# Two 64-row matmuls side by side for the row-maximum scores, and an output added in device memory

## The chip, the cores and the metric

The kernel runs on one core of one Trainium2 chip. The metric is device time in microseconds (us) of one execution. Before the change it is 2181.55 us, the median of three runs (2180.68 to 2182.76).

## The reference

32 samples of 128x1024 float32 pass through four blocks, each of the form x = x + block(layernorm(x)). Cut to what matters:

```
R    = (Wq0 c + bq0) (Wk0 c + bk0)        c: the sample's 128x1024 context; q and k have 64 rows
attn = softmax(R, axis=-1)                1024 x 1024 per sample
x    = x + (attn @ (Wv0 ln(x) + bv0))     block 1
x    = x + (ln(x) * in_scale) @ sign(W).T * out_scale + bias      block 2, scales from a router
x    = x + softmax(ln(x) Wq1 (c Wk1)^T / 32) @ c                  block 3
x    = x + 2 * sum_h score_h * (ln(x) A_h^T) B_h^T                block 4, rank 16, 8 heads
```

## The kernel before

**Stages.** A setup part (until some 130 us) builds products of the weights that all samples share. Then a loop works on three samples at once: iteration k *prepares* sample k (projections, transposes, high and low parts of the operands), does the 1024x1024 *attention* of sample k - 1, and the *chain* of blocks 2 to 4 of sample k - 2. Iterations 3 to 31 are one hardware loop; the first three and the last two are written out. The order of each engine's work is written by hand, and engines wait for one another through semaphores.

**High and low parts.** A 32-bit operand of a product is split into a rounded high part and a remainder, and products are summed from three or four matmuls. `q_hl` holds q's high part in rows 0 to 63 and its remainder in rows 64 to 127; `k_hh` holds k's high part in both halves. `q_m` has a copy of q's high part in rows 64 to 127 (a DMA, L670).

**The row-maximum stage** opens the attention. For each of 8 tiles of 128 queries, `query_scores` (L1114, called at L1183) computes 128x1024 scores with two matmuls (L1125), each 128 rows deep and 512 columns wide, which write the two halves of `scores[t % 2]`. VectorE (DVE) takes the maximum of each row (`row_maximum`, L871 to L876). Query tile t waits for the maximum of tile t - 2. The maxima are transposed (L1222) and enter the second computation of the scores (`key_scores`), from which the exponentials are taken. What is not the row maximum does not depend on these first scores.

**What stands between the query tiles** on TensorE (PE): "key product units" (`keys_through_queries`, L1136 to L1139; three matmuls of 512 columns each, 16 units per sample, the last of the three reads a slot of the ring `m_ring` that SyncE fills from device memory), spread by the table `KW_UNITS` (L611); and the beginning of the chain: transposes of the normalized x (L1105), the gate (L1195, eight products whose outputs are 32 rows each, on four column strips of the array), `fold` (L1216), the router's transpose (L1200), the input scale (L1207), two output scales (L1145).

**The end of a sample.** The last matmuls of block 4 (L1328 to L1334) leave two halves in `shared[0]` and `shared[1]`. VectorE multiplies them by `r_inv[2]`, adds `res` (the sum so far), writes `result` (the same memory as `oscale`) and counts `out_ready` (L1089). SyncE stores `result` to the output (L679). The next iteration's transposes (L1105, at t = 1) write the same `shared` banks, and so wait for `out_ready` (L1187). GpSimd (POOL) waits for `out_ready` too, before it refills `res` with `x1 + bias_rows` (L701). ScalarE (ACT) computes the normalized x for the transposes at the start of the chain (L718, called at L740).

```
for h in range(2):
    last = mm(scores[t % 2][:, half(h)], q_hl[:, t * P:(t + 1) * P], k_hh[:, half(h)], start=True, stop=True)
last.then_inc(maxscores_done, 1)
```

Of the kernel before, what the change touches and what calls it, by code (L numbers as in the profile page):

```python
# [24 lines left out]
P = 128  # L25
# [23 lines left out]
def build(nc, x, ctx_, wq0, bq0, wk0, bk0, wv0, bv0, w_ffn, b_ffn, gate, ics, ocs,  # L49
# [13 lines left out]
    with top:  # L63
# [430 lines left out]
        r_bias = sb("r_bias", [P, 1])  # L494
        r_exp = [sb(f"r_exp{i}", [P, E]) for i in range(2)]
# [107 lines left out]
        out_ready = sem("out_ready")  # L603
        dve_prepare = Steps(sem("dve_prepare"), 2)
# [6 lines left out]
        KW_UNITS = (4, 5, 7, 8, 11, 12, 13, 14, 16)  # L611
# [25 lines left out]
        with nc.Block() as block:  # L637
# [3 lines left out]
            def _(sp):  # L641
# [3 lines left out]
                def body(k, prepare, attend, chain):  # L645
# [31 lines left out]
                    if chain:  # L677
                        sp.wait_ge(out_ready, nth(2, c, 2))
                        sp.dma_start(out[c], result[:, :]).then_inc(stored, 16)  # L679
# [6 lines left out]
            def _(pool):  # L686
# [9 lines left out]
                def body(k, prepare, attend, chain):  # L696
                    b, a, c = k, k - 1, k - 2
                    if chain:
                        pool.wait_ge(x1_ready, nth(2, c, 2))
                        pool.wait_ge(out_ready, nth(2, c - 1, 2))  # L700
                        nc.gpsimd.tensor_tensor(res[:, :], x1[:, :], bias_rows[:, :], ALU.add).then_inc(biased, 1)  # L701
                    if chain:
                        norm_scale(2, c)
                    if prepare:
                        norm_scale(0, b)
                    if chain:
                        norm_scale(3, c)
                    if attend:
                        norm_scale(1, a)

# [4 lines left out]
            def _(act):  # L715
# [20 lines left out]
                def body(k, prepare, attend, chain):  # L736
                    b, a, c = k, k - 1, k - 2
                    if chain:
                        act.wait_ge(xnT_done[3], nth(2, c - 1, 2))
                        normalize(1, c, xn_1, x1)  # L740
# [93 lines left out]
                    if chain:  # L834
# [5 lines left out]
                        nc.scalar.activation(lowT_hi[:, :], shared[1][:, 0:P], ACT.Identity).then_inc(lowT_hi_ready, 1)  # L840

# [4 lines left out]
            def _(dve):  # L846
# [24 lines left out]
                def row_maximum(a, t):  # L871

                    dve.wait_ge(maxscores_done, nth(8, a, t + 1))
# [49 lines left out]
                def body(k, prepare, attend, chain):  # L923
# [6 lines left out]
                    if attend:  # L930
                        row_maximum(a, 1)
                        row_maximum(a, 2)
                    if chain:
# [3 lines left out]
                    if attend:  # L937
                        row_maximum(a, 3)
# [145 lines left out]
                    if chain:  # L1084
                        dve.wait_ge(stored, nth(16, c - 1, 16))
                        dve.wait_ge(lora_scale_ready, nth(1, c, 1))
                        for h in range(2):
                            dve.wait_ge(out_done, nth(2, c, h + 1))
                            nc.vector.scalar_tensor_tensor(result[:, half(h)], shared[h][:, :], r_inv[2][:, :], res[:, half(h)],  # L1089
                                                           ALU.mult, ALU.add).then_inc(out_ready, 1)  # L1090
# [6 lines left out]
            def _(pe):  # L1097
# [16 lines left out]
                def query_scores(a, t):  # L1114
# [9 lines left out]
                    for h in range(2):  # L1124
                        last = mm(scores[t % 2][:, half(h)], q_hl[:, t * P:(t + 1) * P], k_hh[:, half(h)], start=True, stop=True)  # L1125
                    last.then_inc(maxscores_done, 1)
# [52 lines left out]
                def body(k, prepare, attend, chain):  # L1179
                    b, a, c = k, k - 1, k - 2  # L1180
                    for t in range(T):
                        if attend:
                            query_scores(a, t)  # L1183
                        if chain and t == 1:
                            pe.wait_ge(normed[1], nth(1, c, 1))
                            for h in range(2):
                                pe.wait_ge(out_ready, nth(2, c - 1, h + 1))  # L1187
                                transposes(h, xn_1, xnT_done[1])
                        if chain and t == 2:
# [22 lines left out]
                        if attend:  # L1212
                            keys_through_queries(a, range(KW_UNITS[t], KW_UNITS[t + 1]))
                        if chain and t == 2:
                            pe.wait_ge(gate_parts_ready, nth(1, c, 1))
                            mm(shared[0][:, P:P + E], gate_parts[:, :], fold[:, :], start=True, stop=True).then_inc(route_done, 1)  # L1216
                        if chain and t == 6:
                            out_scale(c, 1)
# [141 lines left out]
```

## Time and profile before

| | |
|---|---|
| median of three runs | 2181.55 us |
| the profiled execution's own time | 2182.43 us |
| its span, first to last instruction | 2180.6 us |
| mean granted TensorE clock | 0.988 |
| busy share of the span: PE, DVE, ACT, POOL | 97%, 85%, 53%, 12% |
| DMA: mean busy share of 16 engines | 35.7% |

The profile is of one execution; its own time lies 0.9 us above the median. Busy time of PE counts a matmul from its start to a modelled end, and matmuls overlap, so the start-to-start distance of the records tells what each one costs. Loads of the stationary operand (PEld) are records of their own. In a row of the windows the engines stand in the order PE, PEld, DVE, ACT, POOL. In a row of the timeline, `128*32` after the operands means 128 rows and 32 columns of stationary operand; a matmul on float32 data that is not rounded is recorded as two passes.

### The profile page before, as it was taken

To read this page: it belongs to the slowest core of one execution; us is meant where nothing else is said; L and a number is where in the kernel's file an instruction comes from. 1 tells how busy PE (TensorE), PEld (TensorE's weight loads), DVE (VectorE), ACT (ScalarE), POOL (GpSimd) and SP (SyncE) were. 2 spreads that over 40 slices of the span, in tenths; PEclk is the share of its full clock that TensorE was granted. 3 is DMA by queue.
4 is the path that set the end of the run, shared out by engine and by line. 5 is a ranking of instruction groups with operands and counts; after the bars stand their busy time and mean duration, and the time that the engine had idled before them with its cause. 6 is when DMAs were issued, how large, how long until landed. Compare 5 with 4: busy or idle time off the path is not lost.

```text
span 2180.6 us, 35461 instructions
## 1 busy us (share of the span) xinstructions
PE 2118.4 (97%) x11327; PEld 1660.6 (76%) x11327; DVE 1854.5 (85%) x3099; ACT 1155.2 (53%) x1722; POOL 260.3 (12%) x302
## 2 busy tenths in 40 slices
PE   8889999999999999999999999999999999999985
PEld 6766777778777777787777777877777777777764
DVE  8248989888889898888898988888989888889883
ACT  4125556555555565555555655555556555555551
POOL 0000111111111111111111111111111111111100
PEclk9899999999999999999999999999999999999997
DMA  6453433333433323334333233343333333433300
GB/s 200 145 164 107 133 103 94 115 125 125 135 115 129 103 95 116 125 125 135 115 128 103 95 116 125 125 135 115 126 102 98 116 125 125 135 115 126 105 11 29
DMA packets 110873, 254.02 MB, mean 116 GB/s; under 512 B 12976, under 2 KB 14272, under 8 KB 110848
## 3 DMA queue, kind: packets, MB, share of 16 engines
q1 hardware_dynamic: 110848, 253.69, 35.7%
q8 instruction: 15, 0.25, 0.0%
q14 instruction: 10, 0.08, 0.0%
HBM read 215.89 MB, written 20.97 MB: 109 GB/s over the span
## 4 chain that ended last, share of the span: by engine, by line
PE 83%; DVE 6%; issue 4%; ACT 1%; DVEq 0%; POOL 0%; POOLq 0%; ACTq 0%
PE acc L1176 16%; PE shared L1105 7%; PE shared L1150 6%; PE shared L1151 5%; PE scores L1165 5%; PE scores L1164 5%; PE acc L1136 4%; PE scores L1125 4%; PE acc L1139 4%; PE acc L1137 4%; PE shared L1317 3%; PE shared L1251 3%; PE scores L1272 2%; PE scores L1111 2%; DVE neg_max L875 2%
## 5 line engine op out<-in xcount | busy, mean ns | idle before, releaser
L986 DVE TENSOR_TENSOR p_lo<-prob,p_hi 128x1024 fp32r<-128x1024 f32 x256 | 312.2, 1219 | 103.6 <-ACT p_hi L786 85.7
L779 ACT ACTIVATE prob<-scores 128x1024 f32<-128x1024 f32 x256 | 260.7, 1018 | 241.4 <-PE scores L1165 190.1
L875 DVE TENSOR_REDUCE neg_max<-scores 128x1 f32<-128x1024 f32 x256 | 309.3, 1219 | 45.2 <-PE scores L1125 43.4
L692 POOL TENSOR_TENSOR rstd<-var_eps,minus_half 128x1 f32<-128x1 f32 x128 | 126.1, 985 | 1769.9 <-DVE var_eps L865 1769.9
L786 ACT ACTIVATE p_hi<-prob 128x1024 fp32r<-128x1024 f32 x256 | 271.3, 1060 | 42.7 <-PE acc L1176 38.5
L1136 PE MATMUL acc<-m_hi,cT_hi 128*128 128x512 f32 x512 | 217.6, 425 | 2.2 <-DVE cT_lo L1042 1.3
L1150 PE MATMUL shared<-signT,y_hi 128*128 128x512 f32 x512 | 206.4, 403 | 0.4 <-ACT oscale L768 0.4
L1139 PE MATMUL acc<-m_ring,cT_hi 128*128 128x512 f32 x512 | 202.9, 396 | 0.0
L1164 PE MATMUL scores<-q_hl,k_hh 128*128 128x512 f32 x512 | 201.1, 393 | 1.8 <-DVE q_m L968 1.4
L1137 PE MATMUL acc<-m_hi,cT_lo 128*128 128x512 f32 x512 | 202.4, 395 | 0.0
L1151 PE MATMUL shared<-signT,y_lo 128*128 128x512 f32 x512 | 202.3, 395 | 0.0
L1165 PE MATMUL scores<-q_m,k_l 128*128 128x512 f32 x512 | 202.2, 395 | 0.0
L994 DVE TENSOR_TENSOR p_sum<-p_sum,prob 128x1024 f32<-128x1024 f32 x160 | 194.8, 1218 | 0.0
L1176 PE MATMUL acc<-p_hi,v_hi 128*128 128x512 f32 x512 | 171.2, 416 | 4.4 <-DVE p_lo L986 3.9
L1125 PE MATMUL scores<-k_hh,q_hl 128*128 128x512 f32 x512 | 163.1, 400 | 0.3 <-issue 0.3
L1176 PE MATMUL acc<-p_hi,v_lo 128*128 128x512 f32 x512 | 161.1, 396 | 0.0
L1176 PE MATMUL acc<-p_lo,v_hi 128*128 128x512 f32 x512 | 160.7, 395 | 0.0
L1136 PEld LDWEIGHTS acc<-m_hi,cT_hi 128*128 128x128 f32 x512 | 96.5, 188 | 26.7 <-issue 7.6
L1164 PEld LDWEIGHTS scores<-q_hl,k_hh 128*128 128x128 f32 x512 | 96.1, 188 | 25.4 <-DVE q_m L968 1.6
L1150 PEld LDWEIGHTS shared<-signT,y_hi 128*128 128x128 f32 x512 | 97.0, 189 | 23.2 <-DVE y_lo L905 0.9
L1176 PEld LDWEIGHTS acc<-p_lo,v_hi 128*128 128x128 f32 x512 | 96.0, 188 | 23.5
L1165 PEld LDWEIGHTS scores<-q_m,k_l 128*128 128x128 f32 x512 | 96.1, 188 | 23.0
(215 smaller groups left out, 4184.9 us busy)
## 6 DMA issues: line engine op xcount, KB each, us to landing
m_ring<-m_low SPq DMA_DIRECT2D x512, 256.0 KB, 3.2
c_in<-in_ctx SPq DMA_DIRECT2D x32, 512.0 KB, 3.3
xn<-in_x SPq DMA_DIRECT2D x32, 512.0 KB, 4.1
x<-in_x SPq DMA_DIRECT2D x32, 512.0 KB, 3.2
c_val<-in_ctx SPq DMA_DIRECT2D x32, 512.0 KB, 3.7
out_x<-oscale SPq DMA_DIRECT2D x32, 512.0 KB, 3.0
q_m<-q_hl SPq DMA_DIRECT2D x32, 256.0 KB, 3.1
k_hh<-k_hh SPq DMA_DIRECT2D x32, 256.0 KB, 3.5
```

What stands on the lines that cost most here:

```text
L779: nc.scalar.activation(prob[s % 2][:, :], scores[s % 2][:, :], ACT.Exp).then_inc(exp_ready, 1)
L786: nc.scalar.activation(p_hi[s % 2][:, :], prob[s % 2][:, :], ACT.Identity).then_inc(p_hi_ready, 1)
L875: nc.vector.tensor_reduce(neg_max[:, t:t + 1], scores[t % 2][:, :], AX_X, ALU.max, negate=True).then_inc(row_max, 1)
L986: nc.vector.tensor_tensor(p_lo[s % 2][:, :], prob[s % 2][:, :], p_hi[s % 2][:, :].bitcast(F32), ALU.subtract).then_inc(p_lo_ready, 1)
L1136: mm(acc[:, half(h)], cT_hi[:, f, :], m_hi[:, f, half(h)], start=f == 0, stop=False)
L1137: mm(acc[:, half(h)], cT_lo[:, f, :], m_hi[:, f, half(h)], start=False, stop=False)
L1139: mm(acc[:, half(h)], cT_hi[:, f, :], m_ring[:, u % SLOTS, :], start=False, stop=f == T - 1).then_inc(kw_unit_done, 1)
L1150: mm(shared[h][:, :], y_hi[:, f, :], signT[:, f, half(h)], start=f == 0, stop=False)
L1151: last = mm(shared[h][:, :], y_lo[:, f, :], signT[:, f, half(h)], start=False, stop=f == T - 1)
L1164: mm(scores[s % 2][:, half(h)], k_hh[:, s * P:(s + 1) * P], q_hl[:, half(h)], start=True, stop=False)
L1165: last = mm(scores[s % 2][:, half(h)], k_l1[:, s * P:(s + 1) * P], q_m[:, half(h)], start=False, stop=True)
L1176: last = mm(acc[:, half(h)], v[:, s, :], p[s % 2][:, half(h)], start=first, stop=end)
```

## The change

- `query_scores`: the matmul of half 0 takes rows 0 to 63 of `q_hl` and `k_hh`, that of half 1 rows 64 to 127 of `q_m` and `k_hh`. Both hold the high parts of q and k. The remainder of q no longer enters the first scores. Each counts `maxscores_done`. The built program has these as stationary tiles of 64 rows by 128 columns, at rows 0 and 64 of the array; all other matmuls of the loop are tiles of 128 by 128, or of 128 by 32 (L1195, L1222, L1279).
- The key product units are spread anew (`KW_UNITS`), one unit moves ahead of the gate, and `fold` stands behind the first unit of t = 3.
- The output: SyncE stores `res` when the sum of blocks 1 to 3 is complete (`x3_ready`). ScalarE, instead of VectorE, evicts the last matmuls, scaled by `r_inv[2]`, without adding `res`. GpSimd issues a DMA that adds `result` to the output in device memory, after a one-column multiply that waits for the store.
- VectorE's third row maximum moves ahead of the router's maximum; the two evictions leave VectorE. ScalarE's normalization of x for the chain moves from the start of an iteration to the end of the one before.

```diff
-        KW_UNITS = (4, 5, 7, 8, 11, 12, 13, 14, 16)
+        KW_UNITS = (4, 5, 6, 7, 10, 11, 13, 14, 16)
...
                     if chain:
-                        sp.wait_ge(out_ready, nth(2, c, 2))
-                        sp.dma_start(out[c], result[:, :]).then_inc(stored, 16)
+                        sp.wait_ge(x3_ready, nth(2, c, 2))
+                        sp.dma_start(out[c], res[:, :]).then_inc(res_stored, 16)
...
-                        pool.wait_ge(out_ready, nth(2, c - 1, 2))
+                        pool.wait_ge(res_stored, nth(16, c - 1, 16))
                         nc.gpsimd.tensor_tensor(res[:, :], x1[:, :], bias_rows[:, :], ALU.add).then_inc(biased, 1)
...
+                    if chain:
+                        pool.wait_ge(turned, nth(1, c, 0))
+                        pool.wait_ge(res_stored, nth(16, c, 16))
+                        pool.wait_ge(out_ready, nth(2, c, 2))
+                        nc.gpsimd.tensor_tensor(turn[:, :], minus_half[:, :], minus_half[:, :], ALU.mult).then_inc(turned, 1)
+                        pool.dma_start(out[c], result[:, :], accum_op=ALU.add).then_inc(stored, 16)
...
-                        act.wait_ge(xnT_done[3], nth(2, c - 1, 2))
-                        normalize(1, c, xn_1, x1)
...
+                    if attend:
+                        act.wait_ge(xnT_done[3], nth(2, c, 2))
+                        normalize(1, a, xn_1, x1)
+                    if chain:
+                        act.wait_ge(stored, nth(16, c - 1, 16))
+                        act.wait_ge(lora_scale_ready, nth(1, c, 1))
+                        for h in range(2):
+                            act.wait_ge(out_done, nth(2, c, h + 1))
+                            nc.scalar.activation(result[:, half(h)], shared[h][:, :], ACT.Identity,
+                                                 scale=r_inv[2][:, :]).then_inc(out_ready, 1)
...
-                    dve.wait_ge(maxscores_done, nth(8, a, t + 1))
+                    dve.wait_ge(maxscores_done, nth(16, a, 2 * t + 2))
...
-                        dve.wait_ge(stored, nth(16, c - 1, 16))
-                        dve.wait_ge(lora_scale_ready, nth(1, c, 1))
-                        for h in range(2):
-                            dve.wait_ge(out_done, nth(2, c, h + 1))
-                            nc.vector.scalar_tensor_tensor(result[:, half(h)], shared[h][:, :], r_inv[2][:, :], res[:, half(h)],
-                                                           ALU.mult, ALU.add).then_inc(out_ready, 1)
...
-                    for h in range(2):
-                        last = mm(scores[t % 2][:, half(h)], q_hl[:, t * P:(t + 1) * P], k_hh[:, half(h)], start=True, stop=True)
-                    last.then_inc(maxscores_done, 1)
+                    for h, (q, rows) in enumerate(((q_hl, slice(0, DQK)), (q_m, slice(DQK, P)))):
+                        mm(scores[t % 2][:, half(h)], q[rows, t * P:(t + 1) * P], k_hh[rows, half(h)],
+                           start=True, stop=True).then_inc(maxscores_done, 1)
...
+                        if attend and t == 2:
+                            keys_through_queries(a, range(KW_UNITS[2], KW_UNITS[3]))
                         if chain and t == 2:
...
-                        if attend:
-                            keys_through_queries(a, range(KW_UNITS[t], KW_UNITS[t + 1]))
-                        if chain and t == 2:
+                        if attend and t == 3:
+                            keys_through_queries(a, range(KW_UNITS[3], KW_UNITS[3] + 1))
+                        if chain and t == 3:
                             pe.wait_ge(gate_parts_ready, nth(1, c, 1))
                             mm(shared[0][:, P:P + E], gate_parts[:, :], fold[:, :], start=True, stop=True).then_inc(route_done, 1)
+                        if attend and t != 2:
+                            keys_through_queries(a, range(KW_UNITS[t] + (t == 3), KW_UNITS[t + 1]))
```

**TensorE, query tiles 2 and 3 of the loop, before.** Each row is a matmul, output<-operands (moving, then stationary), with the size of its output.

```order
L1125 MATMUL scores<-k_hh,q_hl 128x512 x2
L1195 MATMUL shared<-xnT,gateT 32x128 x8
L1136 MATMUL acc<-m_hi,cT_hi 128x512
L1137 MATMUL acc<-m_hi,cT_lo 128x512
L1139 MATMUL acc<-m_ring,cT_hi 128x512
L1216 MATMUL shared<-fold,attn 128x8
L1123 REGISTER_ALU
L1125 MATMUL scores<-k_hh,q_hl 128x512 x2
L1136 MATMUL acc<-m_hi,cT_hi 128x512
```

The gate (L1195) follows query tile 2 at once; a unit and `fold` stand between it and query tile 3.

**The same place in the changed program** (L1135 are the query tiles, L1146 to L1149 a unit, L1207 the gate).

```order
L1135 MATMUL scores<-k_hh,q_hl 128x512
L1135 MATMUL scores<-k_hh,q_m 128x512
L1146 MATMUL acc<-m_hi,cT_hi 128x512
L1147 MATMUL acc<-m_hi,cT_lo 128x512
L1149 MATMUL acc<-m_ring,cT_hi 128x512
L1207 MATMUL shared<-xnT,gateT 32x128 x8
L1133 REGISTER_ALU
L1135 MATMUL scores<-k_hh,q_hl 128x512
L1135 MATMUL scores<-k_hh,q_m 128x512
L1146 MATMUL acc<-m_hi,cT_hi 128x512
```

A unit now separates query tile 2 from the gate, and the gate stands directly before query tile 3. It is the one place where two kinds of split array meet; the other seven query tiles have undivided matmuls on both sides.

**GpSimd, end and wrap-around of the loop in the changed program** (L695 and L696 are the normalization scales, L704 the refill of `res`).

```order
L695 TENSOR_TENSOR rstd<-var_eps,minus_half 128x1
L696 TENSOR_TENSOR shift<-neg_mean,rstd 128x1
L715 ISA
L717 TENSOR_TENSOR turn<-minus_half 128x1
L718 ISA
L718 DMA out_x<-oscale 128x1024
L635 REGISTER_ALU
L635 COMPARE_AND_BRANCH
```

Before the change the loop ended after `shift`; the refill of `res` that opens the next iteration now stands behind the adding DMA.

## Rows read from the trace of the kernel before

**Rows 1.** The page, chain of work that ended last, shares of the span.
```profile
PE 83%; DVE 6%; issue 4%; ACT 1%; DVEq 0%; POOL 0%; POOLq 0%; ACTq 0%
```

**Rows 2.** Stretches of an iteration: us, busy us (instructions) by engine, PE clock, DMA share, GB/s.
```profile
1003.12:1019.24 16.12, 15.94 (x91) 12.11 (x89) 14.32 (x22) 4.95 (x12) 2.39 (x1) 1.00 0.75 249
...
sum 62.35, PE 62.15 PEld 48.77 DVE 55.80 ACT 34.92 POOL 8.20; mean PE 20.72 PEld 16.26 DVE 18.60 ACT 11.64 POOL 2.73
```

**Rows 3.** Timeline of PE: start us, us, line, operation, shapes, count [idle <-releaser].
```profile
1003.12 0.63 PE L1125 MATMUL scores<-k_hh,q_hl 128*128 128x512 f32 x2
1003.58 0.39 PE L1136 MATMUL acc<-m_hi,cT_hi 128*128 128x512 f32 x1
...
1004.74 1.25 PE L1105 MATMUL shared<-ident,p_sum 128*128 128x128 f32 x8
1005.75 0.48 PE L1136 MATMUL acc<-m_hi,cT_hi 128*128 128x512 f32 x1
...
1007.24 0.63 PE L1125 MATMUL scores<-k_hh,q_hl 128*128 128x512 f32 x2
1007.80 0.64 PE L1195 MATMUL shared<-xnT,gateT 128*32 128x128 f32 x16
1008.37 0.50 PE L1136 MATMUL acc<-m_hi,cT_hi 128*128 128x512 f32 x1
1008.70 0.39 PE L1137 MATMUL acc<-m_hi,cT_lo 128*128 128x512 f32 x1
```

**Rows 4.** Timeline of PEld, the first stationary load behind the gate.
```profile
1008.37 0.19 PEld L1136 LDWEIGHTS acc<-m_hi,cT_hi 128*128 128x128 f32 x1 [0.20 <-issue]
```

**Rows 5.** Timeline of PE, the two groups of the denominators on four column strips.
```profile
1051.70 0.64 PE L1279 MATMUL scores<-p_sum,ones 128*32 128x256 f32 x8
1052.16 0.61 PE L1279 MATMUL scores<-prob,ones 128*32 128x256 f32 x8
1052.70 1.09 PE L1105 MATMUL shared<-ident,c_in 128*128 128x128 f32 x8
```

**Rows 6.** Timeline of PEld in the setup, from 59.65 us; and the window around it.
```profile
59.49 0.43 PEld L422 LDWEIGHTS setup<-ident,g_nat 16*128 16x128 f32 x3
59.96 0.29 PEld L418 LDWEIGHTS setup<-ident,small 128*128 128x128 f32 x2
...
57.10:60.30 3.20, 3.20 (x20) 3.15 (x20) 0.00 (x0) 0.00 (x0) 0.00 (x0) 0.50 0.98 390
```

**Rows 7.** Timeline of PE, eight transposes that wait for nothing.
```profile
1036.61 1.04 PE L1105 MATMUL shared<-ident,oscale 128*128 128x128 f32 x8
1037.41 0.71 PE L1176 MATMUL acc<-p_hi,v_hi 128*128 128x512 f32 x2
```

**Rows 8.** Timeline of PE, first output scale, and the end of the stage.
```profile
1015.77 0.50 PE L1145 MATMUL shared<-ocs,route3T 96*128 96x512 f32 x1
1016.10 0.40 PE L1136 MATMUL acc<-m_hi,cT_hi 128*128 128x512 f32 x1
...
1018.65 0.40 PE L1139 MATMUL acc<-m_ring,cT_hi 128*128 128x512 f32 x1
1019.24 0.27 PE L1222 MATMUL scores<-ident,neg_max 128*8 128x128 f32 x1 [0.18 <-DVE neg_max L875]
```

**Rows 9.** Timelines of DVE, ACT and POOL in the stage.
```profile
1003.88 1.40 DVE L1089 SCALAR_TENSOR_TENSOR oscale<-shared,r_inv,res 128x512 f32<-128x512 f32 x2
...
1001.74 1.24 ACT L718 ACTIVATE p_sum<-x,shift,rstd 128x1024 f32<-128x1024 f32 x1 [0.23 <-issue]
1005.38 0.60 ACT L734 ACTIVATE xnT<-shared 128x512 f32<-128x512 f32 x1 [2.40 <-PE shared L1105]
...
1012.90 0.58 ACT L758 ACTIVATE x<-acc 128x512 f32<-128x512 f32 x1
...
1005.36 2.39 POOL L701 TENSOR_TENSOR res<-x,bias_rows 128x1024 f32<-128x1024 f32 x1 [3.99 <-DVE oscale L1089]
```

**Rows 10.** DMA issues: tensors, queue, count, KB each, median us to landing.
```profile
out_x<-oscale SPq DMA_DIRECT2D x32, 512.0 KB, 3.0
```

More of the change, by code:

```diff
@@ L494, in build @@
         r_bias = sb("r_bias", [P, 1])
+        turn = sb("turn", [P, 1])
         r_exp = [sb(f"r_exp{i}", [P, E]) for i in range(2)]
@@ L603, in build @@
         out_ready = sem("out_ready")
+        res_stored = sem("res_stored")
+        turned = sem("turned")
         dve_prepare = Steps(sem("dve_prepare"), 2)
@@ L932, in body @@
                         row_maximum(a, 2)
+                        row_maximum(a, 3)
                     if chain:
@@ L936, in body @@
                                                 negate=True).then_inc(r_max_ready, 1)
-                    if attend:
-                        row_maximum(a, 3)
                     if chain:
@@ L1211, in body @@
                             out_scale(c, 0)
-                        if attend:
-                            keys_through_queries(a, range(KW_UNITS[t], KW_UNITS[t + 1]))
-                        if chain and t == 2:
+                        if attend and t == 3:
+                            keys_through_queries(a, range(KW_UNITS[3], KW_UNITS[3] + 1))
+                        if chain and t == 3:
                             pe.wait_ge(gate_parts_ready, nth(1, c, 1))
                             mm(shared[0][:, P:P + E], gate_parts[:, :], fold[:, :], start=True, stop=True).then_inc(route_done, 1)
+                        if attend and t != 2:
+                            keys_through_queries(a, range(KW_UNITS[t] + (t == 3), KW_UNITS[t + 1]))
                         if chain and t == 6:
```

## Prediction

> **What bounds the kernel now.** I read the chain of waits first: 83% of the span is TensorE's own work and only 6% VectorE's [rows 1]. The windows say the same of one iteration: 62.15 us of PE in 62.35; in the row-maximum stage, 1003.12 to 1019.24, PE is busy 15.94 of 16.12 us and DVE 14.32 [rows 2]. So nearly every nanosecond added to or taken from PE's issue, in any stage, counts, and time taken from DVE, ACT or POOL counts only where PE waits for it. The timeline of PE is the view that decides. 
>
> - *Overlap.* The denominators are four 32-column tiles in two passes each: 8 matmuls of 256 columns in 1052.16 - 1051.70 = 0.46 us [rows 5]. One pass over four tiles thus takes 0.23 us, about what a single one must. Divided tiles do run side by side here. I take 0.24 us for the pair instead of 0.46.
> - *Going in.* After the pair at 1007.24 the gate should start at 1007.70 or 1007.71, and starts at 1007.80 [rows 3]: 0.09 us in which the array empties. No engine is named as its releaser.
> - *Coming out.* The second group of denominators takes 0.54 us to its undivided follower, against 0.46 to its like: 0.08 [rows 5]. Behind the gate the load of the next operand has 0.20 us of idle time before it [rows 4] instead of being hidden, and the matmul with it lasts from 1008.37 to 1008.70, 0.33 us for 0.23 [rows 3]: 0.10 for a load of 128 columns in the open. Together about 0.19.
> - *The pair's own load.* It cannot be fetched early either. The gate loads 32 columns; the pair loads 128, so I charge the same 0.10 as behind the gate.
>
> These switches are between 128x128 and 128x32, divided by columns. Is a division by rows as dear? The setup has one: tiles of 16 rows (L422), then tiles of 128 (L418), same operation, no semaphore in between. Three loads of some 0.22 us each begin at 59.49 and end at 59.92, so they step by 0.105; the next was due at 59.81 and comes at 59.96 [rows 6]. So the load is late by 0.15 there too (at a granted clock of 0.50, so I take only the fact from it and the size from rows 3 to 5). It also shows that a load of 16 rows takes a step of 0.105 us: fewer rows do not shorten it.
>
> The Trainium skill, "TensorEngine Tiling (Array Packing)", Key Properties, says that a change of tiling mode, not just of tile, drains TensorE, and names modes by rows and by columns alike; it gives no price. Rows 6 agree for rows, rows 3 and 5 for columns.
>
> A pair will cost 0.09 + 0.10 + 0.24 + 0.09 + 0.10 = 0.62 us against 0.46 or 0.47: **+0.15 us, x256 = +38.4**. The side-by-side streaming wins 0.22, and two switches with two open loads take 0.38.
>
> **The new spread.** The units do not change in number. But the gate now stands directly before query tile 3: one switch and one open load serve both. That saves 0.09 + 0.10 = 0.19 in the 30 or so full iterations: **-5.7**. Nothing else in the spread has a price: PE has no idle time between these rows.
>
> **The output and VectorE.** DVE loses 1.40 us an iteration (L1089) [rows 9], just before its row maxima. That alone is covered by PE, but three small waits of PE go:
>
> - The transposes at t = 1 write the banks that L1089 reads. They take 1005.75 - 1004.74 = 1.01 us [rows 3], against 0.80 where nothing holds them [rows 7]: 0.21. ACT's two evictions take its place. ACT does the normalization from 1001.74 to 1002.98 and then has a gap of 2.40 us before 1005.38 [rows 9]; two evictions of 0.6 us (L734, the same size) end near 1004.2, before PE arrives. Over 30 iterations **-6.3**.
> - The first output scale starts at 1015.77 and holds PE 0.33 us instead of 0.23 [rows 8], since DVE's product comes late and the load stands open. With DVE 1.4 us earlier and one more unit ahead of it: **-3.1**.
> - At the end of the stage L1222 follows 0.59 us behind L1139 [rows 8], where 0.23 + 0.09 (it is a 128x32-mode matmul, so it pays a switch before and after) would do; it waited for the last maximum. 0.27 x 31: **-8.4**. With pairs that last longer DVE is not late again.
>
> POOL's refill of `res` gets behind the store's landing (3.0 us [rows 10]) and the issue of the adding DMA. SyncE can issue the store near 1002.3, behind the same four ring loads; it lands near 1005.4; even with 2 us for POOL's multiply and issue, the refill of 2.39 us [rows 9] ends near 1010, and ACT's L758, which needs it, runs at 1012.90 [rows 9]. Free; if that cover were gone, every microsecond would cost PE the same. The DMA engines are 0.75 busy in the stage at 249 GB/s [rows 2]. The adding DMA brings 0.5 MB, counted once or twice 1.6 or 3.2 us of the 16, so 0.85 to 0.95: the ring's loads still fit, and they are asked for seven units ahead.
>
> At the very end the store of 3.0 us is replaced by POOL's multiply, its issue and an adding DMA, whose price no row shows. Lower bound 0 (as the store), upper bound a read and a write one after the other, 3.0 us more, and 2 us on POOL: I take **+2**, near the lower end since the bytes are the same.
>
> **Sum.** 38.4 - 5.7 - 6.3 - 3.1 - 8.4 + 2 = +16.9 on the execution's own 2182.4: 2199.3. The median lies 0.9 below that execution: 2198.4, rounded **2199 us**, 0.8% slower.
>
> **The rivals.**
>
> *Side by side without a drain* (the other sign). If the 64-row tiles join an undivided stream as its neighbours do, the pair costs 0.23 or 0.24, and loads stay hidden: -0.23 x 256 = -59, with the three waits -18, tail +2: 2107. DVE then decides: without L1089 it has 12.9 us of work in a stage of 16.1 - 1.8 - 0.6 = 13.7, with waits of its own on ACT and PE, so some of it would come back: 2107 to 2135, say 2115. For it speaks the overlap in rows 5; against it the late load in rows 6 and both sides of the gate in rows 3 and 4. It decides from the point where a pair with its surroundings costs under 0.46. The Trainium skill, "TensorE: Matmul & The Clock Gate", Part 3, gives a packed group the duration of one matmul and some 4 ns per further tile; that model is for tiles among themselves and has no term for entering and leaving, and by it alone the time would be this rival's.
>
> *The pair's loads one after the other.* The two halves have 128 columns each. On column strips the loads overlapped, but these are only 32 wide. If the second load waits for the first, the second matmul starts 0.10 later: +26, 2225. Against it: the halves are in different rows.
>
> *A cheaper switch.* If one of the two loads hides behind the emptying array, a pair costs 0.52: +0.05 x 256 = 12.8 in place of 38.4, less the savings: 2173 (2168 to 2182).
>
> *The adding DMA or the later refill holds the ring or ACT.* 1 us an iteration would be +31, 2230; the slack above speaks against it.
>
> **How the numbers follow.** About 0.2% (4.4 us) is what a measurement of this kernel can tell from no change. Forecast (2187 to 2212): 0.57. Loads in series: 0.10. Adding DMA or refill: 0.03. Cheaper switch: 0.10, of it 0.05 within 0.2% of 2181.55. Without a drain: 0.20. So faster 0.25, same 0.06 (with the lower edge of the forecast), slower 0.69. The range holds all but the case without a drain: **2168 to 2230**. The likeliest sign holds most of the chance; the forecast's own range is 2187 to 2212.
>
> **What would show it.** In the profile after: start-to-start from a query tile's first matmul to the unit behind it above 0.4 us; the first matmul of that unit 0.33 long to the next; the record of the query tile's load starting at its own matmul and not 0.2 us ahead; the second matmul of the pair within 0.02 us of the first; the stage about 0.4 us longer than 16.1; L1236 without a wait for DVE; no wait for `out_ready` at the transposes; PE still nearly without idle time. I am wrong if the loads of the 64-row tiles are recorded during the unit before them, or if PE shows waits for ring slots or for `res`.

## The result and the profile after

The changed kernel takes 2200.84 us, the median of 4 runs (2197.91 to 2202.45), against 2181.39 us for the kernel before in 4 runs beside it (2180.68 to 2182.76): a ratio of 1.0082, 95% interval 1.007 to 1.0095. It is 0.8% slower. The prediction was 2199.

| | before | after |
|---|---|---|
| the profiled execution's own time, us | 2182.43 | 2201.21 |
| its span, us | 2180.6 | 2199.5 |
| mean granted TensorE clock | 0.988 | 0.986 |
| start to start of the transposed maxima (L1222, now L1236), median and mean over the loop, us | 62.34, 62.35 | 62.63, 62.69 |

The page after: the busy times, the queue of the adding DMA, the chain's shares, and the two output transfers (last column: us to landing).

```profile
PE 2133.3 (97%) x11327; PEld 1601.5 (73%) x11327; DVE 1823.5 (83%) x3035; ACT 1199.7 (55%) x1786; POOL 298.9 (14%) x366
...
q0 software_dynamic: 4608, 16.78, 4.6%
...
PE 90%; DVE 2%; ACT 1%; issue 1%; POOL 0%; POOLq 0%; DVEq 0%; ACTq 0%
...
out_x<-res SPq DMA_DIRECT2D x32, 512.0 KB, 4.7
out_x<-oscale POOLq DMA_DIRECT2D x32, 512.0 KB, 7.3
```

PE's share of the chain went from 83% [rows 1] to 90% and DVE's from 6% to 2%: the kernel is bound by TensorE more purely than before, and is slower. Of the work that left DVE, PE had waited for the two evictions at the transposes alone, 0.22 us an iteration (output_only, below); the other waits for DVE that are gone went for other reasons.

**The query tile.** PE's timeline, the last matmul of block 4, query tile 0, and the unit behind it:

```profile
1010.40 0.40 PE L1348 MATMUL shared<-bT_hi,lowT_lo 128*128 128x512 f32 x1
1010.73 0.49 PE L1135 MATMUL scores<-k_hh,q_hl 64*128 64x512 f32 x1
1010.73 0.50 PE L1135 MATMUL scores<-k_hh,q_m 64*128 64x512 f32 x1
1011.16 0.50 PE L1146 MATMUL acc<-m_hi,cT_hi 128*128 128x512 f32 x1
1011.50 0.40 PE L1147 MATMUL acc<-m_hi,cT_lo 128*128 128x512 f32 x1
```

And PEld's, the loads of the same matmuls:

```profile
1010.73 0.18 PEld L1135 LDWEIGHTS scores<-k_hh,q_hl 64*128 64x128 f32 x1 [0.37 <-issue]
1010.73 0.18 PEld L1135 LDWEIGHTS scores<-k_hh,q_m 64*128 64x128 f32 x1
1011.16 0.19 PEld L1146 LDWEIGHTS acc<-m_hi,cT_hi 128*128 128x128 f32 x1 [0.24 <-issue]
```

The matmul ahead of the pair takes 1010.73 - 1010.40 = 0.33 us instead of 0.23 or 0.24: the array empties. The pair takes 1011.16 - 1010.73 = 0.43: a load in the open, one stream of 0.24 for both halves, and the array empties again. The next matmul takes 0.34 to its follower instead of 0.23, since its load too is open. Both halves start at 1010.73, and so do both their loads; the loads' records carry the idle time in front of them. Before, a pair of 0.46 had none of this [rows 3].

The Trainium skill, "TensorEngine Tiling (Array Packing)", Key Properties, says that a change of tiling mode drains TensorE. This trace agrees for row halves, with 0.09 us on each side. It shows no such drain at the transpose of the maxima, which the built program has as a tile of 128 by 32 and the trace records as 128*8; whether the array counts so small a tile as a mode of its own no run here shows:

```profile
1025.69 1.23 DVE L892 TENSOR_REDUCE neg_max<-scores 128x1 f32<-128x1024 f32 x1
...
1026.83 0.40 PE L1149 MATMUL acc<-m_ring,cT_hi 128*128 128x512 f32 x1
...
1026.97 0.08 PEld L1236 LDWEIGHTS scores<-ident,neg_max 128*8 128x8 f32 x1 [0.18 <-DVE neg_max L892]
1027.06 0.27 PE L1236 MATMUL scores<-ident,neg_max 128*8 128x128 f32 x1
...
1027.09 0.47 PE L1160 MATMUL shared<-signT,y_hi 128*128 128x512 f32 x1
```

It follows its forerunner after 0.23 us, with nothing for emptying, and the next starts 0.03 later. Before, the same two steps took 0.59 and 0.10 [rows 8]. DVE ends its last maximum at 1026.92, before L1149 has streamed, so PE loses nothing to it.

**The end of the program.** The timeline of all engines from the last evictions; the span ends at 2199.5:

```profile
2190.66 0.63 PE L1348 MATMUL shared<-bT_hi,lowT_lo 128*128 128x512 f32 x1
...
2191.32 0.69 ACT L856 ACTIVATE oscale<-shared,r_inv 128x512 f32<-128x512 f32 x1 [0.51 <-PE shared L1348]
2192.18 0.19 POOL L717 TENSOR_TENSOR turn<-minus_half 128x1 f32<-128x1 f32 x1 [13.63 <-ACT oscale L856]
2192.64 0.89 POOL L718 DMA_DIRECT2D out_x<-oscale  x1 [0.27 <-issue]
```

From the end of the last matmul, 2191.29, to the end of the span are 8.2 us. Before, they were 3.8 (2176.16 + 0.63 to 2180.6): +4.4. Of it 3.9 is the adding DMA, 2192.64 to 2199.5 or 6.9 us, where the plain store takes 3.0 [rows 10].

### The profile page after: what moved, and what is told of

Same layout as the page of the kernel before. It is cut to its first block, busy times and chain, and to the rows that moved or that the text cites. A ratio compares the mean times of both kernels' runs of the same rounds, so it can differ in the third digit from the quotient of the medians.

```text
span 2199.5 us, 35791 instructions
## 1 busy us (share of the span) xinstructions
PE 2133.3 (97%) x11327; PEld 1601.5 (73%) x11327; DVE 1823.5 (83%) x3035; ACT 1199.7 (55%) x1786; POOL 298.9 (14%) x366
## 3 DMA queue, kind: packets, MB, share of 16 engines
q0 software_dynamic: 4608, 16.78, 4.6%
## 4 chain that ended last, share of the span: by engine, by line
PE 90%; DVE 2%; ACT 1%; issue 1%; POOL 0%; POOLq 0%; DVEq 0%; ACTq 0%
PE acc L1186 16%; PE shared L1115 7%; PE acc L1146 7%; PE shared L1160 5%; PE shared L1161 5%; PE acc L1147 5%; PE acc L1149 5%; PE scores L1175 5%; PE scores L1174 5%; PE scores L1135 5%; PE shared L1331 3%; PE shared L1265 3%; PE scores L1286 2%; PE scores L1121 2%; PE shared L1219 2%; PE scores L1293 1%
## 5 line engine op out<-in xcount | busy, mean ns | idle before, releaser
L695 POOL TENSOR_TENSOR rstd<-var_eps,minus_half 128x1 f32<-128x1 f32 x128 | 129.1, 1009 | 1680.0 <-DVE var_eps L882 1680.0
L1146 PE MATMUL acc<-m_hi,cT_hi 128*128 128x512 f32 x512 | 231.1, 451 | 3.3 <-DVE cT_lo L1058 2.4
L1149 PE MATMUL acc<-m_ring,cT_hi 128*128 128x512 f32 x512 | 202.7, 396 | 0.0
L1146 PEld LDWEIGHTS acc<-m_hi,cT_hi 128*128 128x128 f32 x512 | 97.9, 191 | 44.8 <-issue 34.9
L1135 PE MATMUL scores<-k_hh,q_hl 64*128 64x512 f32 x256 | 127.4, 498 | 0.3 <-issue 0.3
L1135 PE MATMUL scores<-k_hh,q_m 64*128 64x512 f32 x256 | 127.1, 497 | 0.0
```

The lines of the kernel that those rows point to most:

```text
L1135: mm(scores[t % 2][:, half(h)], q[rows, t * P:(t + 1) * P], k_hh[rows, half(h)], start=True, stop=True).then_inc(maxscores_done, 1)
L1146: mm(acc[:, half(h)], cT_hi[:, f, :], m_hi[:, f, half(h)], start=f == 0, stop=False)
L1149: mm(acc[:, half(h)], cT_hi[:, f, :], m_ring[:, u % SLOTS, :], start=False, stop=f == T - 1).then_inc(kw_unit_done, 1)
```

## The experiments

Each time is a median of its own runs. The ratios are to runs of the kernel before on the same chip as each, whose medians were 2183.4 to 2183.8 us, about 2 more than in the first comparison; so ratios and periods are compared, not bare times.

### Undoing one part, and doing one part

**whole_pairs**: the changed kernel with the query tiles as before.

```diff
-                    for h, (q, rows) in enumerate(((q_hl, slice(0, DQK)), (q_m, slice(DQK, P)))):
-                        mm(scores[t % 2][:, half(h)], q[rows, t * P:(t + 1) * P], k_hh[rows, half(h)],
-                           start=True, stop=True).then_inc(maxscores_done, 1)
+                    for h in range(2):
+                        last = mm(scores[t % 2][:, half(h)], q_hl[:, t * P:(t + 1) * P], k_hh[:, half(h)], start=True, stop=True)
+                    last.then_inc(maxscores_done, 1)
```

> The changed kernel with the query tiles as before: undivided pairs of 128-row matmuls; the new spread, the output by ScalarE and the adding DMA stay. Theory (two switches of the array and two loads in the open per tile): each pair falls from 0.62 us with its surroundings to 0.47, less the switch that the gate shares: 0.15 x 256 - 6 = 33 us faster than the changed kernel, so 2166 to 2172, also faster than the kernel before. Rival (the output path or the spread costs the time, the tiles are free): stays at 2200.

Measured: 2178.96 us (12 runs), ratio 0.9983 (0.9974 to 0.9991), period 62.00. The output path and the spread alone make a kernel that is a little faster, but slower than expected: 2172 beside 2181.4 would be a ratio of 0.9957, so I missed by about 6 us. The timeline of all engines at the end of the stage shows one reason:

```profile
1013.74 1.22 DVE L892 TENSOR_REDUCE neg_max<-scores 128x1 f32<-128x1024 f32 x1
...
1014.61 0.40 PE L1149 MATMUL acc<-m_ring,cT_hi 128*128 128x512 f32 x1
...
1015.01 0.08 PEld L1236 LDWEIGHTS scores<-ident,neg_max 128*8 128x8 f32 x1 [0.45 <-DVE neg_max L892]
```

The transpose of the maxima follows 0.40 behind L1149, so PE waits 0.17 for the last maximum; with the divided tiles it does not. There is a second one: query tile 4 takes 0.57 us to the router's transpose behind it (1007.16 to 1007.73) where a pair that waits for nothing takes 0.46, since that transpose waits for the router's chain on DVE. The tiles cost 62.63 - 62.00 = 0.63 an iteration, not the 1.0 that 8 pairs less one shared switch make, since undividing brings such waits back.

**tiles_only**: the kernel before with the divided tiles, the output and the spread as before (the reverse of that diff, and DVE's count).

> The kernel before with the 64-row tiles alone; spread, order and output as before. Theory: +0.15 x 256 = +38, less what VectorE's waits at L1222 shrink by (0.1 to 0.3 us in 31 iterations): 2211 to 2220. Rival (output path costs): within 0.2% of 2181. Rival (tiles gain): 2125 or less.

Measured: 2191.34 us (5 runs), ratio 1.0037 (1.0024 to 1.005), period 62.59. I missed by 20 us. PE's timeline has the same transposes, and the end of the stage:

```profile
1010.44 1.09 PE L1105 MATMUL shared<-ident,p_sum 128*128 128x128 f32 x8
1011.28 0.48 PE L1136 MATMUL acc<-m_hi,cT_hi 128*128 128x512 f32 x1
...
1024.71 0.40 PE L1139 MATMUL acc<-m_ring,cT_hi 128*128 128x512 f32 x1
1024.95 0.27 PE L1222 MATMUL scores<-ident,neg_max 128*8 128x128 f32 x1
```

The transposes take 1011.28 - 1010.44 = 0.84 us (0.85 in the median of the loop) and L1222 comes after 0.24, as in the full change, though DVE still evicts the output. These waits for DVE vanish because PE comes later, not because DVE comes earlier.

**output_only**: the kernel before with the new output path, with whole pairs and the old spread (the rest of the diff).

> The kernel before with the output path of the change alone (store of res, ScalarE's evictions, adding DMA, normalization at the end of the iteration). Theory: the transposes' wait (0.16 us) and the wait for the last maximum (up to 0.4 us) go in 30 iterations, the tail grows by 4 us: 2167 to 2178. Rival (the second DMA or the later refill of res costs): 2185 or more.

Measured: 2181.20 us (11 runs), ratio 0.999 (0.9982 to 0.9999), period 62.10. The expectation, 2178 at most beside 2181.4 or a ratio of 0.9984, is missed too, though narrowly. One wait goes and one stays, in PE's timeline:

```profile
1001.06 1.03 PE L1116 MATMUL shared<-ident,p_sum 128*128 128x128 f32 x8
1001.85 0.47 PE L1147 MATMUL acc<-m_hi,cT_hi 128*128 128x512 f32 x1
...
1014.78 0.39 PE L1150 MATMUL acc<-m_ring,cT_hi 128*128 128x512 f32 x1
1015.33 0.27 PE L1233 MATMUL scores<-ident,neg_max 128*8 128x128 f32 x1 [0.17 <-DVE neg_max L892]
```

The transposes fall to 0.79, as reasoned. The transposed maxima still come 0.55 behind the unit. DVE's timeline tells why:

```profile
1009.99 1.23 DVE L892 TENSOR_REDUCE neg_max<-scores 128x1 f32<-128x1024 f32 x1
1011.13 1.28 DVE L972 TENSOR_TENSOR xnT<-xnT,shared 128x512 f32<-128x512 f32 x2
1012.33 1.22 DVE L892 TENSOR_REDUCE neg_max<-scores 128x1 f32<-128x1024 f32 x1
1013.46 0.68 DVE L922 TENSOR_TENSOR y_lo<-xnT,y_hi 128x512 fp32r<-128x512 f32 x1
1014.06 1.22 DVE L892 TENSOR_REDUCE neg_max<-scores 128x1 f32<-128x1024 f32 x1
```

From the maximum of query tile 5 on DVE works without a gap: the input scale's two products, maximum 6, a remainder, maximum 7. That row starts when PE delivers query tile 5, so 1.4 us less work on DVE at the start of the stage does not move its end.

| period, us; ratio | whole pairs | 64-row tiles |
|---|---|---|
| output as before | 62.34; 1 | 62.59; 1.0037 |
| new output path | 62.10; 0.999 | 62.63; 1.0082 (with the new spread) |

The parts do not add. The tiles cost 0.25 an iteration on the old output path and 0.53 on the new one (0.63 with the same spread on both sides, against whole_pairs); the output path saves 0.24 with whole pairs. With the tiles it saves nothing that shows, which leaves its longer tail as a net loss; but that corner of the table has the new spread too, and the tiles with the new output path and the old spread were not run.

The new spread, with the order around the gate and of DVE's third maximum, is worth little: with whole pairs it takes the period from 62.10 to 62.00. The first output scale takes 0.34 us to its follower in output_only and 0.24 in whole_pairs; the wait for the last maximum is some 0.15 shorter there (0.55 and 0.40 behind the unit), and query tile 4's wait for the router 0.11 longer.

### Is it the overlap or the switch?

**same_rows**: both halves of a pair from rows 0 to 63, which hold the same high parts. **twice**: each pair issued twice, back to back; only the second counts.

```diff
# same_rows
-                    for h, (q, rows) in enumerate(((q_hl, slice(0, DQK)), (q_m, slice(DQK, P)))):
+                    for h, (q, rows) in enumerate(((q_hl, slice(0, DQK)), (q_hl, slice(0, DQK)))):
# twice
+                    for last in (False, True):
...
+                            if last:
+                                one.then_inc(maxscores_done, 1)
```

> The changed kernel with both matmuls of a tile on rows 0 to 63 (same operands' high parts, same result). The switches stay, the streaming side by side goes. Theory: +0.21 to 0.23 us x 256 = +54 to +59 over the changed kernel: 2254 to 2260. Rival (the two halves did not overlap in the changed kernel either): no difference, 2200. With loads of the second in the open as well: 2280.

> The changed kernel with each 64-row pair issued twice in a row (same data, same place, the second writes over the first; counted once). Theory (the cost is in entering and leaving the divided array, not in the pair): one more pair inside costs only its streaming, 0.24 us x 256 = +61 over the changed kernel, about 2262. Rival (each pair pays for itself, 0.62 us): +159, 2360. Rival (the second pair's loads stand in the open, 0.10 each): +87, 2288.

Measured: 2256.84 us (2 runs; 1.0338, 1.032 to 1.0356) and 2259.43 us (2 runs; 1.0347, 1.0328 to 1.0366), both as expected. PE's timeline, same_rows, then twice:

```profile
1035.56 0.73 PE L1135 MATMUL scores<-k_hh,q_hl 64*128 64x512 f32 x2
1036.22 1.09 PE L1115 MATMUL shared<-ident,p_sum 128*128 128x128 f32 x8
```

```profile
1035.56 0.49 PE L1136 MATMUL scores<-k_hh,q_hl 64*128 64x512 f32 x1
1035.56 0.50 PE L1136 MATMUL scores<-k_hh,q_m 64*128 64x512 f32 x1
1035.89 0.39 PE L1136 MATMUL scores<-k_hh,q_hl 64*128 64x512 f32 x1
1035.90 0.39 PE L1136 MATMUL scores<-k_hh,q_m 64*128 64x512 f32 x1
1036.22 0.50 PE L1149 MATMUL acc<-m_hi,cT_hi 128*128 128x512 f32 x1
```

On the same rows the pair takes 0.66: the second half streams after the first. Side by side it takes 0.43, and a second pair behind it adds only 0.23 (0.66 for both). So the overlap is whole, and all of the cost is in entering and leaving. The divided halves also count `maxscores_done` once each, where a whole pair counted once. That has no price that shows: in twice the first pair counts nothing, and in adjacent, below, both pairs count, and two pairs take 0.66 or 0.67 us in either.

### Fewer switches

**adjacent**: query tile 4 directly behind query tile 3, so that one switch serves the gate and both.

```diff
-                        if attend:
+                        if attend and t != 4:
                             query_scores(a, t)
+                        if attend and t == 3:
+                            query_scores(a, 4)
```

> The changed kernel with query tile 4 moved directly behind query tile 3, so that the gate, tile 3 and tile 4 share their switches. Theory: one exit with its open load and one entry with its open load go, 0.38 us less the load between the pairs if it cannot be hidden (0.10), in 31 iterations: 9 to 12 us under the changed kernel, 2189 to 2192. Rival (the switch is hidden by VectorE's row maxima anyway): within 0.2% of the changed kernel, 2197 to 2205.

Measured: 2200.54 us (5 runs), ratio 1.0075 (1.0061 to 1.0088), period 62.62: no gain. The time is the rival's, though not for the rival's reason. The waits of the trace (engine and line, released by, us in total, times, longest), and PE's timeline:

```profile
PEld shared L1214 <- DVE route L963: 19.3, 32, 1.7
```

```profile
1017.87 0.40 PE L1149 MATMUL acc<-m_ring,cT_hi 128*128 128x512 f32 x1
1018.36 0.32 PE L1214 MATMUL shared<-ident,route 128*96 128x128 f32 x1
```

By PE's timelines the two tiles save 0.32 an iteration: with their borders they take 1.09 in the changed kernel and 0.77 here. But the router's transpose now stands closer to the gate and has to wait for the router's chain on DVE and ACT. Its load is idle for 0.6 us an iteration in the row above, which overstates what is lost, since PE still streams L1149 for part of it: L1149 takes 0.49 to its follower where it would take 0.23, so PE loses 0.26 there, and 0.04 more behind it, about what was saved. In the changed kernel the same row has 10.6 us in total, 0.24 in most iterations, and that is only the open load behind query tile 4.

**adjacent_covered**: that order, one unit moved from behind query tile 5 to ahead of the router's transpose, and the last output as in old_tail below.

```diff
-        KW_UNITS = (4, 5, 6, 7, 10, 11, 13, 14, 16)
+        KW_UNITS = (4, 5, 6, 7, 11, 12, 13, 14, 16)
```

> As adjacent (tile 4 directly behind tile 3), with the last sample's output the old way, and one unit of 0.70 us moved from between tiles 5 and 6 to between the tile pair and the router's transpose. Theory: what adjacent saved (0.38 us of switch and open load an iteration) came back as TensorE's wait for the router's chain on DVE (0.6 us an iteration); a unit in front of it covers that wait, so the period falls from 62.62 to 62.25 to 62.40 and the time to 2183 to 2189 (2194.98 of the old tail, less 0.22 to 0.38 x 31). Rival: DVE is late as such after the pair of tiles (its maxima of 1.22 us against pairs that come 0.33 apart), and the wait turns up at a later tile or at the transpose of the maxima: the period stays at 62.6, the time at 2193 to 2196. In neither case does it beat the undivided pairs with the old tail.

Measured: 2183.95 us (10 runs), ratio 1.0003 (0.9993 to 1.0013), period 62.37. The same wait:

```profile
PEld shared L1227 <- DVE route L969: 1.7, 1, 1.7
```

It is gone but for the first time, and the period is 0.27 below old_tail's 62.64. This order and the old tail together take back the whole loss of the change, 17 us by the ratios (1.0082 to 1.0003). By the traces 4.4 of it is the tail, and some 10 the loop (1.3 of them the one long iteration): one switch fewer, and a unit in front of the wait that would have swallowed it.

### The tail, and a faster kernel

**old_tail**: the changed kernel, with the last sample stored as before.

```diff
+                        if attend:
+                            sp.wait_ge(x3_ready, nth(2, c, 2))
+                            sp.dma_start(out[c], res[:, :]).then_inc(res_stored, 16)
+                        else:
+                            sp.wait_ge(out_ready, nth(2, c, 2))
+                            sp.dma_start(out[c], result[:, :]).then_inc(last_stored, 16)
...
-                    if chain:
+                    if chain and attend:
```

(and DVE's two evictions for that sample.)

> The changed kernel with the last sample's output as before (VectorE adds res, SyncE stores), all others by the adding DMA. Theory: the tail behind the last matmul shrinks from 8.2 to 3.8 us: 2196 to 2197. Rival (the tail is longer for the clock alone): 2200.

Measured: 2194.98 us (4 runs), ratio 1.0054 (1.0038 to 1.0069). A little less than expected. By the ratios the old tail is worth 0.0028 x 2184 = 6 us. The traces say where that comes from: from the end of the last matmul to the end of the span it is now 2193.1 - 2189.2 = 3.9 us instead of 8.2, so 4.4 less (4.35 before rounding); most of the rest lies ahead of the loop, where the two programs are the same (first transposed maxima at 154.6 and 156.2). So 4.4 is the tail's price.

**best**: whole pairs, the new output path with the old tail, and three units behind query tile 7.

```diff
-        KW_UNITS = (4, 5, 6, 7, 10, 11, 13, 14, 16)
+        KW_UNITS = (4, 5, 6, 7, 10, 11, 12, 13, 16)
```

> Undivided pairs, the change's output path with the last sample's output as before, and one more key product unit behind query tile 7 (KW_UNITS 4, 5, 6, 7, 10, 11, 12, 13, 16). Theory: 4.4 us of tail under whole_pairs, and the wait for the last row maximum (0.17 us and more, 30 iterations) covered by the unit: 4 to 8 us; together 2167 to 2172 beside a kernel before of 2182. Rival (the unit's place changes nothing since PE only waits elsewhere): 2174 to 2176.

Measured: 2172.58 us (5 runs, 2169.78 to 2176.65), ratio 0.9952 (0.9938 to 0.9965), period 61.92. PE's timeline at the end of the stage:

```profile
1013.05 0.39 PE L1162 MATMUL acc<-m_ring,cT_hi 128*128 128x512 f32 x1
1013.28 0.27 PE L1249 MATMUL scores<-ident,neg_max 128*8 128x128 f32 x1
```

The last maximum is covered by a third unit, and the transposed maxima follow after 0.23. This beats both kernels. By its ratio it is at the slow end of what I expected (2172 beside 2182 is 0.9954). The unit gives less than the 0.17 and more that I had counted on, 0.08 us an iteration: it was taken from behind query tile 5, and the first output scale, which it had covered in whole_pairs, waits again (0.34 us to its follower instead of 0.24). The other 4.4 of the 6.8 us by which it beats whole_pairs are the tail.

## Why the prediction was right, and which terms were not

The forecast was that the switches cost more than the overlap wins, and that nothing else gives back as much. Both hold. Term by term:

- *The pairs, +0.15 us each.* Right, by its parts: 0.62 expected; 0.09 or 0.10 more ahead, 0.43, and 0.11 more behind measured, 0.63. That divisions by rows and by columns cost the same was the step with the thinnest evidence, and it held. Loads of the two row halves start together, so the rival with serial loads falls; the 0.33 ahead of the pair and the 0.34 behind it exclude the rivals without a drain and with a cheaper one. One step of the way there was weaker than it was put: that 0.23 us for a pass of 256 columns is "about what a single one must" [rows 5]. No row has such a pass alone, and 512 rounded columns take 0.23 [rows 3], so rows 5 show that tiles overlap but not that they do so wholly. That they do is shown by same_rows and twice.
- *The gate's shared switch, -0.19.* Right. PE's timeline has 0.58 us for the gate, as before [rows 3], and the next pair starts right behind it:

```profile
1015.52 0.65 PE L1207 MATMUL shared<-xnT,gateT 128*32 128x128 f32 x16
1016.10 0.50 PE L1135 MATMUL scores<-k_hh,q_hl 64*128 64x512 f32 x1
```

  But the old order with the tiles would have had a shared switch too, behind query tile 2 (the gate follows at once). This is no merit of the new spread.
- *Transposes, -0.21.* The wait is gone: 1.01 to 0.85, in which the open load behind query tile 1 lies. The reason, ACT in place of DVE, is shown by output_only. It was not needed here: tiles_only has the same 0.85.
- *Output scale, -0.10.* It still takes 0.34, now for the open load that its neighbour, query tile 6, leaves, which was already in the 8 pairs. The sum was right and the row did not change. tiles_only has it too. Of the two reasons given, DVE being earlier does nothing by itself (0.34 in output_only); with the unit ahead of the scale as well the wait goes, if the pairs are whole (0.24 in whole_pairs, and 0.34 again in best, where that unit is elsewhere). "Nothing else in the spread has a price" was right only because this was already counted here.
- *The end of the stage, -0.27.* The size and the reason were off. It gave 0.43 in this iteration, from 0.59 + 0.10 to 0.23 + 0.03, and 0.40 in the median of the loop. I had charged L1236 a switch that it does not pay. "With pairs that last longer DVE is not late again" was the right half of the reason; the lead of DVE, 1.4 us, does nothing here, by output_only. In tiles_only, with the old spread, the row of DVE's work that begins at query tile 5 has PE's own work against it, 1019.00 to 1024.95, or 5.95 us; before it was 1013.23 to 1019.24 with 0.35 of waiting in it, so 5.66. The borders of three tiles make up nearly the whole wait.
- *Tail, +2.* Too small: +4.4, in the trace of the change and in that of old_tail. I took the lower end of 0 to 5, "since the bytes are the same". An adding DMA of 512 KB lands in 7.3 us and the store in 3.0, so the upper end was the better choice.
- *What I had not priced.* From the first matmul of the v projection (L1121) to L1331 behind it are 2.01 us instead of 1.92 to L1317. The 16 matmuls of the projection step by 0.11 as before; the excess lies between the last of them and L1331, whose load has 0.23 us of idle time ahead of it (released by "issue"). tiles_only has it and whole_pairs has not, so it comes with the tiles; the cause stays open.
- *Cover of the refill.* It held for ACT's L758, which was asked about, and not for DVE, which was not. The refill began 1005.36 - 1003.12 = 2.24 us into the stage [rows 9, 3], and now 1015.66 - 1010.73 = 4.93. POOL's timeline:

```profile
1014.45 0.20 POOL L717 TENSOR_TENSOR turn<-minus_half 128x1 f32<-128x1 f32 x1 [5.57 <-DMA out_x<-res]
1015.02 0.91 POOL L718 DMA_DIRECT2D out_x<-oscale  x1 [0.38 <-issue]
1015.66 2.69 POOL L704 TENSOR_TENSOR res<-x,bias_rows 128x1024 f32<-128x1024 f32 x1
```

  Here it ends at 1018.35, just before DVE's product for the router, which takes 0.23 us. In the iteration of 63.95 us it came later, and the two overlapped. DVE's timeline of that iteration, then of the one above, and POOL's of the long one:

```profile
328.39 1.38 DVE L959 TENSOR_SCALAR route<-r_exp,r_inv 128x8 f32<-128x8 f32 x1
...
1018.59 0.23 DVE L959 TENSOR_SCALAR route<-r_exp,r_inv 128x8 f32<-128x8 f32 x1
```

```profile
327.06 2.67 POOL L704 TENSOR_TENSOR res<-x,bias_rows 128x1024 f32<-128x1024 f32 x1
```

  The product ends at 329.77, 0.04 us behind the refill. The two share no tensor, and the trace doesn't say what holds the product, but this is not by chance: whenever its record is longer than 0.23 (6 of 32 times here, 12 in whole_pairs, 17 in best), it ends 0.04 behind the refill's end. The kernel before and tiles_only, whose refill is over long before, have it at 0.23 every time. The router's transpose then made PE wait 1.0 of the 1.3 us that this iteration lost; in the other five PE lost at most 0.05. PE's idle time ahead of that transpose, without the 1.6 us of the first sample that every kernel has, is 2.2 us in whole_pairs and 2.3 in best. So the later refill has a price, small and not in every iteration, and best isn't free of it.

The terms by themselves would give +0.43 an iteration in the loop, which came at +0.29 (median) to +0.34 (mean), and +2 for the tail, which came at +4.4. In the spans, 10.5 us of the 18.9 lie in the loop where some 13 were forecast (0.43 in 31 iterations), 4.4 in the tail where 2 was, and 4.0 outside both (2.5 ahead and 1.5 behind), of which the sum had only the pairs that stand there. These misses offset each other: 2199 against 2200.84 is closer than the terms deserve, and in part luck. The stage lasts 16.33 us (1010.73 to 1027.06) instead of 16.12, where 0.4 more was forecast. The deeper fault, which the sum hides, is that I credited three waits to the output path. Of the three it removes one, the transposes', and only with whole pairs; tiles_only shows that the tiles absorb that one and the one at the end of the stage by themselves. Had the prediction been asked of either part alone, it would have been wrong, as my expectations for tiles_only and output_only were.

## What to carry to other kernels

Price a divided array by its borders: here emptying and an open load on each side, 0.38 us together, against 0.23 won by a pair of 512 columns. Two adjacent pairs would pay (0.85 us with both borders, worked out from twice, against 0.93; an estimate) if nothing waits behind them; so group divided tiles before dividing any, and put work in front of the wait that the saved time runs into. Where a chain on another engine is only just late, added TensorE time is partly free and removed TensorE time partly lost: price a change by its combination, not part by part, and count each wait once. An operation moved to a later place on an idle engine isn't free either: look at what the other engines run there. And a fixed tail matters: here the adding DMA at the very end cost 4.4 us, and storing the last sample plainly gave them back.

## What the runs showed of the hardware that I had not expected

- Around a transpose with a stationary operand of 128x8 amid 128x128 matmuls no emptying shows (0.23 to it, 0.03 behind it), while the gate's 128x32 group and the 64x128 pairs do (0.09 each time).
- A small product on DVE that meets a 128x1024 addition on POOL ends 0.04 us behind it, whatever was left of the addition (1.38 us instead of 0.23 at worst in the changed kernel).
- The adding DMA of 512 KB lands in 7.3 us (median of 32, 5.2 to 8.3) against 3.0 for the plain store, and in 6.9 as the last transfer of the program. The share of the added queue is 4.6% of the DMA engines' time for 16.78 MB. The store of `res` in mid-iteration takes 4.7 instead of 3.0, and `c_val` 5.5 instead of 3.7.
- The stretches with half the clock, between 124 and 144 us and in the last 51 to 73 us, come at somewhat different times in each kernel. The time ahead of the loop differs by 1.6 us between the changed kernel and old_tail, whose programs are the same there, about as much as a small edit gives.
